# Graph aggregate of a three-step gated unit: the adjacency becomes the weight of a wide product, placed a frame ahead, and its result is turned back by VectorE and a trip through HBM

## The reference, cut to what matters

```python
h = x
for _ in range(3):
    a  = einsum('nm,bmd->bnd', adj, h)             # a_in and a_out: the same matrix is given for both
    av = concatenate([a, a], axis=-1)
    z  = sigmoid(av @ w3.T + b3 + h @ u3.T + c3)
    r  = sigmoid(av @ w4.T + b4 + h @ u3.T + c3)
    hv = tanh(av @ w5.T + b5 + (r * h) @ u5.T + c5)
    h  = (1 - z) * h + z * hv
out = layernorm(x + h, axis=-1)
```

## Time and profile before

| | before |
|---|---|
| median of three timed runs | 758.65 us |
| the profiled execution, whole | 758.45 us |
| its span, first to last instruction | 755.8 us |
| TensorE busy | 746.7 us, 99% |
| VectorE busy | 545.3 us, 72% |
| ScalarE busy | 388.1 us, 51% |
| GpSimd busy | 72.4 us, 10% |
| mean granted TensorE clock | 0.997 of full speed |

### The profile page before, as it was taken

How to read it: one execution, slowest core, us unless ns; L and a number is a source line. 1 busy time by engine, 2 the same in 40 slices (tenths; PEclk the granted TensorE clock), 3 DMA queues, 4 the chain that set the end, 5 groups by cost and what they waited for, 6 DMA issues and landing times.

```text
span 755.8 us, 10483 instructions
## 1 busy us (share of the span) xinstructions
PE 746.7 (99%) x3684; PEld 632.5 (84%) x3684; DVE 545.3 (72%) x863; ACT 388.1 (51%) x647; POOL 72.4 (10%) x89
## 2 busy tenths in 40 slices
PE   9999999999999999999999999999999999999995
PEld 8888888888888888888888888888888888888884
DVE  5657787777767776787767766887677765888577
ACT  5545454455556453554556544545456544545455
POOL 0000111100110011110100001120000000121002
PEclk9999999999999999999999999999999999999998
DMA  8122412223453322222355331221335522121223
GB/s 310 33 39 35 91 28 34 37 46 81 110 129 67 91 53 36 36 40 57 63 121 120 85 89 31 37 38 30 64 64 120 139 63 37 31 36 28 40 38 118
DMA packets 208569, 51.82 MB, mean 69 GB/s; under 512 B 201248, under 2 KB 201376, under 8 KB 208544
## 3 DMA queue, kind: packets, MB, share of 16 engines
q1 hardware_dynamic: 208400, 51.24, 31.4%
q10 hardware_dynamic: 144, 0.26, 0.1%
HBM read 18.95 MB, written 8.39 MB: 36 GB/s over the span
## 4 chain that ended last, share of the span: by engine, by line
PE 98%; DVE 0%; issue 0%; POOL 0%; ACT 0%; POOLq 0%; DVEq 0%
PE ps_g L347 17%; PE ps_g L348 17%; PE ps_g L349 17%; PE ps_v L347 11%; PE ps_v L349 11%; PE ps_v L348 11%; PE ps_a L376 11%; PE ps_g L434 1%; PE ps_g L473 1%; PE ps_v L434 0%; DVE dz L845 0%; PE ps_a L509 0%; DVE hT L848 0%; POOL rstd L914 0%; ACT z L651 0%
## 5 line engine op out<-in xcount | busy, mean ns | idle before, releaser
L564 ACT ACTIVATE ps_v<-ps_v,bias 128x512 f32<-128x512 f32 x96 | 63.6, 662 | 201.0 <-PE ps_v L349 201.0
L347 PE MATMUL ps_g<-aT_hi,wt_lo 128*128 128x512 f32 x376 | 146.3, 389 | 0.0
L348 PE MATMUL ps_g<-aT_lo,wt_hi 128*128 128x512 f32 x376 | 146.3, 389 | 0.0
L349 PE MATMUL ps_g<-aT_hi,wt_hi 128*128 128x512 f32 x376 | 146.3, 389 | 0.0
L701 DVE TENSOR_TENSOR dz<-ps_v,hT 128x512 f32<-128x512 f32 x64 | 44.1, 691 | 103.3 <-ACT ps_v L564 103.3
L594 ACT CAST rh_hi<-rh 128x512 fp32r<-128x512 f32 x94 | 58.3, 621 | 77.8 <-DVE rh L721 77.8
L602 ACT ACTIVATE z<-ps_g,bias 128x512 f32<-128x512 f32 x94 | 62.7, 685 | 44.7 <-PE ps_g L349 44.2
L696 DVE TENSOR_TENSOR aT_lo<-ps_a,aT_hi 128x512 fp32r<-128x512 f32 x96 | 62.5, 674 | 28.9 <-ACT aT_hi L549 28.8
L349 PEld LDWEIGHTS ps_g<-aT_hi,wt_hi 128*128 128x128 f32 x376 | 70.6, 188 | 14.7
L348 PEld LDWEIGHTS ps_g<-aT_lo,wt_hi 128*128 128x128 f32 x376 | 70.6, 188 | 14.7
L347 PEld LDWEIGHTS ps_g<-aT_hi,wt_lo 128*128 128x128 f32 x376 | 70.6, 188 | 14.6
(11 more groups left out here) (92 smaller groups left out, 1188.8 us busy)
## 6 DMA issues: line engine op xcount, KB each, us to landing
hn<-hb SPq DMA_DIRECT2D x736, 32.0 KB, 2.0
x_in<-in_x_rows SPq DMA_DIRECT2D x15, 512.0 KB, 5.1
xT<-in_x_cols SPq DMA_DIRECT2D x15, 512.0 KB, 4.4
out<-y SPq DMA_DIRECT2D x15, 512.0 KB, 3.1
wide<-in_w_t SPq DMA_DIRECT2D x3, 512.0 KB, 6.5
x_in<-in_x_rows SPq DMA_DIRECT2D x2, 256.0 KB, 3.6
xT<-in_x_cols SPq DMA_DIRECT2D x2, 256.0 KB, 5.1
out<-y_tail SPq DMA_DIRECT2D x2, 256.0 KB, 2.2
```

The lines of the kernel that those rows point to most:

```text
L347: nc.tensor.matmul(dst, lhs_lo, rhs_hi, start=first, stop=False, skip_group_check=True)
L348: nc.tensor.matmul(dst, lhs_hi, rhs_lo, start=False, stop=False, skip_group_check=True)
L349: return nc.tensor.matmul(dst, lhs_hi, rhs_hi, start=False, stop=last, skip_group_check=True)
L564: nc.scalar.activation(ps_v[:, oc, :], ps_v[:, oc, :], ACT.Tanh, bias=bias[:, BV, oc:oc + 1]).then_inc(v_ready, 1)
```

## The change

- `aggregate` becomes a product of split operands: `adjT_hi` and `adjT_lo` are the weights, and all of h nodes-first, 1024 columns, streams through in two halves of 512 columns with three matmuls each. ScalarE makes `hn_hi` and VectorE `hn_lo` for it.
- The result is now nodes-first in `ps_a` and has to be turned: VectorE turns its 32x32 blocks out of PSUM into `ab` (`transpose_a`, last in its frame), SyncE writes `ab` to a buffer in HBM with one DMA (`park_a`), waits, and reads it back block-permuted with four DMAs (`move_a`) into `aT`, which ScalarE and VectorE split with `a_high` and `a_low` as before, now out of SBUF.
- It is placed a frame ahead: in frame j TensorE does `second_half(j)`, the u product of j+1, the aggregate of j+2, the candidate of j.
- h goes the same way by HBM: `hb` is laid out by quads, `park_h` writes it with one DMA, SyncE waits, `move_h` reads it with four DMAs of 128 KB into `hn`, in place of the sixteen SBUF-to-SBUF DMAs.
- `add_x` goes from GpSimd to VectorE; the normalisation goes from behind tanh to the end of ScalarE's frame; `x_rows` is stored in the new order of `hn`. Frames 0 and 1 keep the old aggregate.

The core of the diff:

```diff
+    turned_h = [nc.dram_tensor(f"turned_h{k}", [P, QUADS, LINE], F32).ap() for k in range(2)]
+    turned_a = nc.dram_tensor("turned_a", [P, QUADS, LINE], F32).ap()
+        def by_block(t):
+            return t[:, :, :].rearrange("p q (x i) -> p q x i", i=BLK)
+        def quads_first(t):
+            return t[:, :, :].rearrange("p c (b q s) -> p q (c b) s", q=QUADS, s=BLK)
...
# SyncE
-            def move(i, j):
-                sp.wait_ge(hb_ready, frames(i, j))
-                for n in range(QUADS):
-                    for f in range(QUADS):
-                        sp.dma_start(hn[...][n * BLK:(n + 1) * BLK, :, :, f * BLK:(f + 1) * BLK],
-                                     hb[j % 2][f * BLK:(f + 1) * BLK, :, :, n, :]).then_inc(moved[j % SLOTS], DMA)
+            def park_h(i, j):
+                sp.wait_ge(hb_ready, frames(i, j))
+                sp.dma_start(turned_h[j % 2], hb[j % 2][:, :, :]).then_inc(hb_parked[j % 2], DMA)
+            def move_h(i, j):
+                sp.wait_ge(hb_parked[j % 2], parks(i, j))
+                for n in range(QUADS):
+                    sp.dma_start(hn[j % SLOTS][n * BLK:(n + 1) * BLK, ...],
+                                 turned_h[j % 2][:, n, :].rearrange("(f r) x -> r f x", f=QUADS))\
+                      .then_inc(moved[j % SLOTS], DMA)
+            def park_a(i, j):
+                sp.wait_ge(ab_ready, split_aggregates(i, j))
+                sp.dma_start(turned_a, ab[:, :, :]).then_inc(ab_parked, DMA)
+            def move_a(i, j, first=False):
+                sp.wait_ge(ab_parked, DMA * split_aggregates(i, j))
+                if not first:
+                    sp.wait_ge(a_lo_ready, 2 * frames(*frame_before(i, j)))
+                for f in range(QUADS):
+                    sp.dma_start(aT[f * BLK:(f + 1) * BLK, :, :],
+                                 turned_a[:, f, :].rearrange("(n r) x -> r n x", n=QUADS)).then_inc(a_moved, DMA)
# SyncE's frame: reload_rows or store, then
+                    park_h(bi, bj); move_h(bi, bj)
+                    park_a(*after(i, j, 2)); move_a(*after(i, j, 2))
+                    load_cols(...) (four frames of twelve), reload_rows(...) (frames 4 and 5)
...
# TensorE
+            def aggregate(i, j, first=False):
+                pe.wait_ge(hn_hi_ready, split_aggregates(i, j))
+                pe.wait_ge(hn_lo_ready, split_aggregates(i, j))
...
+                for k in range(2):
+                    cols = slice(k * ROWS, (k + 1) * ROWS)
+                    product(ps_a[:, k, :], adjT_hi[:, :], adjT_lo[:, :], hn_hi[:, cols], hn_lo[:, cols],
+                            True, True).then_inc(a_ready, 1)
+            def frame(i, j, carry):
+                second_half(i, j, carry)
+                update_product(*after(i, j, 1), carry)
+                aggregate(*after(i, j, 2))
+                candidate(i, j)
...
# ScalarE: frame = tanh, h_high and sigmoid r (twice), then
+                if second and not first:
+                    hn_high(*second)          # waits on x_loaded or moved, 128x1024
                 (rh_high twice, sigmoid z twice)
+                    a_high(*following)        # waits on a_moved, 128x1024
+                if j == FR - 1: normalise(i, 0)   # or normalise(i - 1, j + 1), moved here
...
# VectorE: frame = new h, times_r twice, then
+                    for c in range(C):
+                        h_low(*following, c)
+                    hn_low(*second)           # 128x1024
                 (rh_low twice)
                 transpose_blocks(bi, bj, ...)  # now reads quads_first(hT)
+                    a_low(*following)         # 128x1024
                 statistics(...)
+                if before and SLOTS <= bj < 2 * SLOTS:
+                    add_x(bi, bj)
+                if second:
+                    transpose_a(*second, first=first)   # waits on a_ready, 128x1024 out of PSUM
...
# GpSimd
-            def add_x(i, q): ...
```

More of the change, by code:

```diff
@@ L329, in _ @@
             for j in range(EARLY, FR - 1):
-                frame(last, j, True, False)
+                frame(last, j, True, False, second=j + 2 < FR)
             for q in (0, 2, 1):
@@ L357, in dense, with first_aggregate @@
                 return done
[L359 to L367, removed]
+            def first_aggregate(j):
+                if j == 1:
+                    pe.wait_ge(rows_second, DMA)
                 for hf in range(2):
-                    if first:
+                    if j == 0:
                         pe.wait_ge(rows_first[hf], DMA)
@@ L605, in frame @@
                     weight_high(U5)
-                if following:
-                    split_first_half(*following)
+                    act.wait_ge(adjT_loaded, DMA)
+                    nc.scalar.copy(adjT_hi[:, :], adjT[:, :]).then_inc(adj_hi_ready, 1)
+                    for hf in range(2):
+                        first_a_high(1, hf)
+                    hn_high(*second)
+                elif following:
+                    a_high(*following)
+                if j == FR - 1:
+                    normalise(i, 0)
+                elif carry and j < SLOTS - 1:
+                    normalise(i - 1, j + 1)
             def weight_high(k):
@@ L733, in h_low, with frame @@
                                         ALU.subtract).then_inc(hT_lo_ready, 1)
[L735 removed]
+            def frame(i, j, carry, following, second, first=False):
                 before = carry or j > 0
@@ L757, in frame @@
                     weight_low(U5)
+                    dve.wait_ge(adj_hi_ready, 1)
+                    nc.vector.tensor_tensor(adjT_lo[:, :], adjT[:, :], f32(adjT_hi[:, :]),
+                                            ALU.subtract).then_inc(adj_lo_ready, 1)
+                    for hf in range(2):
+                        first_a_low(1, hf)
+                    hn_low(*second)
                 if before and following:
                     transpose_blocks(bi, bj, carry or bj >= 2)
+                if following and not first:
+                    a_low(*following)
                 if j >= FR - 2:
@@ L895, in _ @@
             pool.wait_ge(neg_half_ready, 1)
-            for q in range(SLOTS):
-                add_x(0, q)
             with pool.Fori(1, ROUNDS) as i:
@@ L901, in _ @@
                     scale_and_shift(i - 1, q)
-                for q in range(SLOTS):
-                    add_x(i, q)
             last = ROUNDS - 1
```

236 lines of the change are left out of this document (150 added, 86 removed).

## The result

The changed kernel takes **738.97 us** (median of four runs, 738.83 to 739.15) beside 758.48 us for the kernel before (758.26 to 761.08, run with it): a ratio of 0.9735, with an interval of 0.9714 to 0.9757. That is 2.6% faster. The forecast was 738.4 us in a range of 736.5 to 754. The profiled execution took 739.15 us, of which 737.4 are the span.

The account below looks back on a forecast made before the run. TensorE, busy for 99% of the span, was taken to bound the kernel. The profiled 758.45 us minus 20.2 for 46 shorter aggregates, all else hidden, gives 738.2; 0.2 added for the median makes 738.4, range 736.5 to 754.

Parts of the forecast that it names:

- TensorE's part: Aggregates of frames 2 to 47: 1.80 us becomes 1.36, a frame 14.96 us, 46 x 0.44 = 20.2 us less.
- The fourth rival: New aggregate's product misses the others' pitch: at 0.30 us a matmul, six take 1.80 and time stays 758; chance 0.04.
- VectorE's part: VectorE's work of 12.2 us a frame, 13.2 with statistics and add_x spread over twelve, stays hidden under 14.96.
- the third rival: VectorE becomes the bound: block-stepping transpose_blocks and a_low at half rate need 15.6 us a frame, 768 in all; chance 0.03.
- the mean of 13.9 us: VectorE's mean frame if its 2.2 us wait beside add_x stays in four frames of twelve; still under 14.96.
- The trip of h: From VectorE's turned h through HBM into hn: lands at 3.1 us of a frame, before the r sigmoid's end at 3.6.
- L: Time from VectorE having turned h until move_h has landed: 8.7 us (6.5 to 14.1).
- SyncE's part: SyncE's single queue of parks, issues and a load takes 13.5 us a frame against 14.96.
- one frame a round goes over, and eleven recover 1.5 us each: SyncE's queue, frame 0 of a round: two more issues up to 0.8 us, a park meeting loads up to 3.3 more.
- the ring: From h's landing to the next hb takes 4.8 us, so a frame lasts at least L + 4.8 = 13.5; takes over at L = 10.2.
- The first rival: Frames with 512 KB loads or stores stall: some 27 lose 0.1 to 0.5 us, start 2 us, 741 to 754; chance 0.14.
- The start: First frames: transpose_a(0, 2) delays the first v_minus_h to 28.9 us; cost nothing, up to 2 us if group 2's rows come late.

Follow-up runs that it names:

- Experiment 1: Kernel before the change with half of the old aggregate (eight of sixteen float32 matmuls) left out in frames 2 to 47; 716.71 us, 0.9444.
- experiment 9: Changed kernel with add_x back on GpSimd, nothing else; 742.13 us, 0.9771 of the kernel before.
- Experiment 4: Changed kernel with one spare 512 KB write of hb to HBM, waited for, ahead of each park_h; 780.65 us, 1.0303 of the kernel before.
- Experiments 6 and 7: Changed kernel with one and two spare hb writes ahead of each park, loads and stores in the rounds cut to a sixteenth of their bytes; 742.4 and 838.63 us.
- experiments 1 and 12: Experiment 1, and the changed kernel with x_nodes kept as the whole of x, rows 64 KB apart as before; the latter 738.58 us.
- experiments 2 and 4: Changed kernel with one matmul pass in place of three in the new aggregate, 701.48 us; and Experiment 4.
- experiment 5: Changed kernel with two spare 512 KB writes of hb, waited for, ahead of each park_h; 897.55 us, 1.1827 of the kernel before.

## Why the prediction was right, and where it was not

**TensorE's part** held to the last digit: pitch, 1.36 us, 14.96 us a frame, 46 times, no idle time before u, the aggregate or gate_r. Experiment 1 shows the old aggregate's price from the other side. The fourth rival is out.

**VectorE's part** held. A round of twelve frames has 158.42 us of work, 13.2 a frame, the figure of the prediction; a quiet one 12.28. The groups of the kernel after:

```profile
L649 ACT CAST hn_hi<-hn 128x1024 fp32r<-128x1024 f32 x32 | 33.4, 1044 | 3.1 <-DMA hn<-turned_h 3.1
...
L817 DVE TENSOR_TENSOR aT_lo<-aT,aT_hi 128x1024 fp32r<-128x1024 f32 x46 | 56.4, 1226 | 35.3 <-ACT aT_hi L639 35.3
L807 DVE STREAM_TRANSPOSE ab<-ps_a 128x1024 f32<-128x1024 f32 x46 | 57.4, 1248 | 21.7 <-PE ps_a L421 20.6
```

Stepping through blocks of 32 costs nothing (1.23 to 1.25 us for 1024 elements, SBUF or PSUM), so the third rival is out. The add of 1220 ns on VectorE took the place of a wait of 2.2 us, as assumed; experiment 9 shows that the other way round would not have been hidden, though the mean of 13.9 us that the prediction gave for it is under 14.96. That step was too easy, and not because the mean runs over twelve frames: in the four frames concerned VectorE is busy for 14.4 us, still under 14.96. What counts is where the 2.2 us falls, against the 2.3 us of slack that the prediction itself gave h_low. The GPSIMD Engine Reference of the Trainium skill (section Specifications), on GpSimd contending with VectorE, is borne out by the 2.2 us, here and in the earlier trace rows.

**The trip of h** was hidden with more room than predicted. From hb (426.85) the measured parts are 0.03 to the issue, 2.64 for the park (3.1 was taken), 1.30 to the last of four issues of 0.43 (0.65 was taken each), and 3.0 for its landing: L = 7.0, not 8.7. "SBUF — State Buffer" of the Trainium skill (section "Door 1: The DMA port swizzle") would have made L 9.9 by the estimate given. L stayed under both. As an estimate, 128 KB at that page's 218 GB/s takes 0.60 us; the issues themselves are 0.43 us apart, so the rule could show itself here by no more than 0.7 us, and no run tells.

**SyncE's part** was right in outcome: parks of 2.64 and 3.78 us where 3.1 and 4.75 were taken. It waits for hb 185.6 / 46 = 4.0 us a frame on average, so its own work in a frame takes 11.0 us, not 13.5.

**Where the prediction's reasoning failed,** without showing in the time: "one frame a round goes over, and eleven recover 1.5 us each", and the threshold at which the ring "makes the kernel slower than before at L = 10.6". Experiment 4 has L = 9.6, a ring of 14.4, and is 22 us slower than before. Two things are missing from the step. One is that the ring of h isn't the only path: the trip of the aggregate waits in the same queue behind the trip of h, and it is this one that TensorE waits for in the long frames of experiment 4 (aT_lo ahead of gate_r). The prediction had it "two us ahead of gate_r" in every frame; it is 3.6 us ahead in a quiet frame of the kernel after, 1.8 in its tightest, and 3.55 late in experiment 4. The other is that a ring isn't judged by its quiet length alone. When a load delays a park by 3 to 5 us, VectorE's lateness goes only at 14.96 minus the ring per frame: 3.2 us a frame in the kernel after (ring 11.8), where the one frame of 15.43 us between two transposes is followed by one of 14.49, and 0.5 in experiment 4, where the next loads come first. How the 42 us divide between the two, no run tells. Experiments 6 and 7 take most of the load bytes away, and the formula holds again. The first rival, with its place in frames with loads, was the right thing to fear; 2.64 us on the trip would have brought it, at a price beyond its range.

**The start** was costed at nothing with 2 us as its bound; it took 0.8. The first cast of h waits for its data until 8.12 us in the profiled execution, against 7.18 in the kernel before, and the first loads land 0.8 to 1.1 us later by their medians (xT 5.9 in place of 5.1, the nodes-first image 4.7 in place of 3.6). It is not the wait for v_minus_h that the prediction named. In the eleven profiled executions of kernels with the new start (experiments 1 and 12 have another) the cast stood anywhere from 7.44 to 8.42, in the two with the old start at 6.82 and 7.18; why is open. The 0.2 us that the forecast added from the profiled execution to the median came out the other way (738.97 is 0.18 under 739.15), so the forecast is only 0.6 us off where start and tail alone cost 1.0, and that much is luck.

## What to carry to other kernels

When one engine is the bound in every frame, the gain of a change to it can be read off its pitch; the work goes into showing that everything added returns in time. Write each cycle that a new wait closes as a ring, and ask two things of it: its length in a quiet frame, and what it wins back in a frame after the longest delay that the trace shows. Follow also whatever stands behind the new wait in the same queue up to the engine that is the bound, and take its slack in the most loaded frame: that is used up long before the ring is full. And don't average a stall over the frame: set it against the slack at the place where it falls.

## What the hardware showed unasked

- A DMA from SBUF to SBUF costs its queue 0.63 us to issue with 32 runs of 1 KB, and 0.65 with the shorter runs of before, though it moves only 32 KB; one of 128 KB from HBM to SBUF costs 0.43, and one of 512 KB 0.33 to 0.43. Going through HBM was cheaper than going straight: L = 7.0 against 11.4 us.
- The same 512 KB write lands in 2.6 us in a quiet queue, 5.8 behind two transfers of its size, 7.9 behind three (experiments 2 and 4).
- Behind some of TensorE's longer waits (3.55 us in experiment 4, 2.6 to 7.4 in experiment 5, but not behind two of 3.1 us in experiment 4) the granted clock was 0.50 to 0.55 for 2 to 5 us, and 512 columns took 0.43 us in place of 0.23. Such a wait costs more than its own length.
- ScalarE rounds 1024 elements in one instruction in 1.04 us, where two of 512 take 1.14 to 1.24.
